# First attention of a Flamingo-like kernel: scores in two row halves, masks of four heads, maximum subtracted on VectorE

## The reference

```
def _feature_map(x, fm_w, fm_b):
    z = jnp.einsum('nshd,ed->nshe', x, fm_w) + fm_b
    return jnp.concatenate([jnp.exp(z), jnp.exp(-z)], axis=-1)   # 8 -> 16 per head
# query = layernorm(x): 128 rows; keys = values = context: 77 rows; 16 heads
v, k, q = (_feature_map(x, fm_w, fm_b) for x in (v, k, q))
scores = jnp.einsum('nqhd,nkhd->nhqk', q, k) / jnp.sqrt(jnp.float32(EMBED))
attn = jax.nn.softmax(scores, axis=-1)
out = jnp.einsum('nhql,nlhd->nqhd', attn, v)
return out.reshape(N, S, HEADS * EXP_DIM) @ fc_w.T + fc_b
# x = x + tanh(g_xattn[0]) * (the above)
```

## Time and profile before

| | |
|---|---|
| three runs | 2557.52, 2557.7, 2568.71 us; median 2557.7 |
| profiled execution | 2560.78 us, span 2559.0 us |
| busy over the span | TensorE 2374.1 us (93%), VectorE 1993.7 (78%), ScalarE 1637.5 (64%), GpSimd 1541.8 (60%) |
| mean granted clock of TensorE | 0.947 of full speed |

### The profile page before, as it was taken

The page is one execution under the profiler, slowest core; times in us unless marked ns, Lnnn a source line. Parts: engine busy times, 40 slices in busy tenths (PEclk is TensorE's granted clock), DMA queues, the critical chain, the costliest instruction groups (busy, mean ns, idle before and its releaser), DMA issues. The chain is left out here.

```text
span 2559.0 us, 87168 instructions
## 1 busy us (share of the span) xinstructions
PE 2374.1 (93%) x29830; PEld 1817.8 (71%) x29830; DVE 1993.7 (78%) x4882; ACT 1637.5 (64%) x3917; POOL 1541.8 (60%) x1166
## 2 busy tenths in 40 slices
PE   4999999969599999999985999999999996699999
PEld 3888888847366666666654888888888886466666
DVE  6999999969788888888885666656565666888888
ACT  4888888834356555555654666666666653488887
POOL 2333333325366666666655777777777762488888
PEclk9999999955799999999997999999999996799999
DMA  2000000020422222222214333333343431000000
GB/s 75 6 5 5 6 5 6 4 66 0 87 88 82 86 83 79 87 80 86 76 34 104 63 63 59 64 58 66 57 67 57 67 58 39 3 10 12 12 12 17
DMA packets 411273, 123.96 MB, mean 48 GB/s; under 512 B 366195, under 2 KB 381171, under 8 KB 410432
## 3 DMA queue, kind: packets, MB, share of 16 engines
q1 hardware_dynamic: 278816, 89.38, 15.2%
q10 hardware_dynamic: 132384, 33.63, 5.9%
HBM read 109.03 MB, written 13.89 MB: 48 GB/s over the span
## 5 line engine op out<-in xcount | busy, mean ns | idle before, releaser
L1086 POOL TENSOR_TENSOR f_low<-f_hidden,f_high 128x512 f16<-128x512 f32 x336 | 442.5, 1322 | 250.4 <-ACT f_high L1021 248.6
L1044 DVE TENSOR_TENSOR f_hidden<-f_hidden,f_share 128x512 f32<-128x512 f32 x336 | 374.5, 1115 | 0.0
L1638 POOL TENSOR_TENSOR a_q_head_high<-a_q_t_high,a_head_mask 128x2048 f16<-128x2048 f16 x64 | 232.7, 3635 | 200.4 <-PE a_score L1424 192.3
L1230 POOL TENSOR_TENSOR f_low<-f_hidden,f_high 128x512 f16<-128x512 f32 x256 | 296.6, 1159 | 71.2 <-ACT f_high L1173 71.0
L398 POOL TENSOR_TENSOR a_kfeat<-a_feat,a_head_mask 128x616 f32<-128x616 f32 x128 | 154.1, 1224 | 302.2 <-ACT a_feat L333 302.2
L1027 ACT ACTIVATE f_act_out<-f_gate 128x512 f32<-128x512 f32 x336 | 200.4, 596 | 194.7 <-PE f_gate L991 194.7
L1067 DVE SCALAR_TENSOR_TENSOR f_hidden<-f_up,f_act_out 128x512 f32<-128x512 f32 x336 | 229.9, 684 | 83.0 <-PE f_up L991 59.8
L1021 ACT ACTIVATE f_high<-f_hidden 128x512 f16<-128x512 f32 x336 | 210.5, 627 | 73.0 <-DVE f_hidden L1044 71.6
L1573 ACT ACTIVATE a_prob<-a_score 128x308 f32<-128x308 f32 x256 | 109.4, 427 | 224.0 <-PE a_score L1432 224.0
L1730 DVE TENSOR_REDUCE a_score<-a_score 128x4 f32<-128x308 f32 x256 | 123.8, 484 | 161.9 <-PE a_score L1424 161.9
L1001 PE MATMUL f_y<-w_down_high,f_high 128*128 128x128 f16 x1344 | 242.4, 219 | 2.2 <-POOL f_low L1086 2.2
(11 more groups left out here) (273 smaller groups left out, 9327.0 us busy)
## 6 DMA issues: line engine op xcount, KB each, us to landing
f_share<-expert_shares SPq DMA_DIRECT2D x128, 256.0 KB, 3.2
a_q_pos<-queries ACTq DMA_DIRECT2D x64, 512.0 KB, 4.1
f_share<-expert_shares SPq DMA_DIRECT2D x128, 128.0 KB, 3.0
relative_values<-a_rel_all SPq DMA_DIRECT2D x1024, 4.0 KB
x_all<-in_x SPq DMA_DIRECT2D x4, 1024.0 KB, 7.7
f_share<-expert_shares SPq DMA_DIRECT2D x128, 32.0 KB, 1.8
queries<-a_q_parts SPq DMA_DIRECT2D x64, 64.0 KB, 3.5
a_rel<-relative_values SPq DMA_DIRECT2D x64, 64.0 KB, 1.9
```

The lines of the kernel that those rows point to most:

```text
L1044: nc.vector.tensor_tensor(hidden[r][:, :], hidden[r][:, :], share[k][:, :, :].rearrange("p t q -> p (t q)"), ALU.mult).then_inc(scaled, 1)
L1086: nc.gpsimd.tensor_tensor(low[r][:, :], hidden[r][:, :], high[r][:, :], ALU.subtract).then_inc(low_ready, 1)
L1230: nc.gpsimd.tensor_tensor(low[k][:, :], hidden[k][:, :], high[k][:, :], ALU.subtract).then_inc(low_ready, 1)
L1638: nc.gpsimd.tensor_tensor(q_head[p][k][:, :, :], q_t[p][k][:, :].unsqueeze(2).broadcast_to([P, P, NH]), head_mask[:, :].unsqueeze(1).broad ...
```

## The change

Row halves: rows 0 to 63 of a chunk hold four heads, rows 64 to 127 the other four. `own_mask`, the sum of the two halves of `head_mask`, lets kfeat be four heads wide instead of eight: each row keeps its head's place within its own half. One `scores(n, p, c)` then issues two matmuls that contract 64 rows each, in the two row halves of the array, into the two score banks. All four quarters get their maximum subtracted by VectorE into `prob`, and one exp each. `normalize` moves from VectorE to ScalarE, as scale and shift, where `layernorm_constants` makes the shift with one more instruction. The orders of all engines but GpSimd are written anew. One small operation and one count of `weights_ready` come before the loops.

```
-        kfeat = [sb(f"kfeat{p}", [P, 2, 8, KC]) for p in range(2)]
+        kfeat = [sb(f"kfeat{p}", [P, 2, HQ, KC]) for p in range(2)]
...
-                def scores(n, p, u):
-                    if inside(n, 0, B):
-                        if u % 2 == 0:
-                            pe.wait_ge(kfeat_ready, 2 * n + u // 2 + 1)
-                        wait(pe, exped, 4 * n + u - 1)
-                        c = u // 2
-                        nc.tensor.matmul(score_ps[u % 2][:, 0:QW], feat[p][:, c, 0:P],
-                                         kfeat[p][:, c, 4 * (u % 2):4 * (u % 2) + 4, :],
-                                         start=True, stop=True).then_inc(score_ready, 1)
+                def scores(n, p, c):
+                    if inside(n, 0, B):
+                        pe.wait_ge(kfeat_ready, 2 * n + c + 1)
+                        wait(pe, shifted, 4 * n + 2 * c)
+                        for r in range(2):
+                            own = slice(HALF * r, HALF * (r + 1))
+                            nc.tensor.matmul(score_ps[r][:, 0:QW], feat[p][own, c, 0:P], kfeat[p][own, c, :, :],
+                                             start=True, stop=True).then_inc(score_ready, 1)
...
                 def slot(n, p):        # TensorE
                     o = 1 - p
                     scores(n, p, 0)
-                    turn(n - 1, 2)
+                    turn(n - 1, 3)
+                    mix(n - 1, o, 1)
                     prep_z(n + 1, o)
-                    mix(n - 1, o, 0)
                     fin_project(n - 3, o)
                     scores(n, p, 1)
-                    turn(n - 1, 3)
                     prep_value(n, p)
-                    mix(n - 1, o, 1)
-                    scores(n, p, 2)
+                    mix(n - 1, o, 2)
                     turn(n, 0)
-                    mix(n - 1, o, 2)
+                    mix(n - 1, o, 3)
+                    turn(n, 1)
                     fin_turn(n - 2, p)
+                    turn(n, 2)
+                    mix(n, p, 0)
                     prep_turn(n + 2, p)
-                    scores(n, p, 3)
-                    turn(n, 1)
-                    mix(n - 1, o, 3)
...
                 def exp(n, u):         # ScalarE
                     if inside(n, 0, B):
-                        act.wait_ge(shift_ready, 4 * n + u + 1)
-                        if u in ON_DVE:
-                            last = nc.scalar.activation(prob[u][:, :, :], prob[u][:, :, :], ACT.Exp, scale=SCALE)
-                        else:
-                            wait(act, prob_ready, 4 * n + u - 3)
-                            for h in range(HQ):
-                                last = nc.scalar.activation(prob[u][:, h, :], score_ps[u % 2][:, KC * h:KC * (h + 1)],
-                                                            ACT.Exp, bias=shift[u][:, h:h + 1], scale=SCALE)
-                        last.then_inc(exped, 1)
+                        act.wait_ge(shifted, 4 * n + u + 1)
+                        nc.scalar.activation(prob[u][:, :, :], prob[u][:, :, :], ACT.Exp, scale=SCALE).then_inc(exped, 1)
...
+                def normalize(n, p):
+                    if inside(n, 0, B):
+                        wait(act, xn_t, n - 1)
+                        nc.scalar.activation(xn[p][:, :], x_all[:, n, :], ACT.Identity, bias=xn_shift[:, n, :],
+                                             scale=rstd[:, n, :]).then_inc(xn_ready, 1)
...
                 def slot(n, p):        # ScalarE
                     o = 1 - p
                     high_prob(n - 1, 2)
+                    copy_xn(n + 1, o)
+                    high_prob(n - 1, 3)
+                    exp(n, 0)
+                    exp(n, 1)
                     features(n + 1, o)
-                    exp(n, 0)
-                    high_prob(n - 1, 3)
                     high_value(n, p)
-                    exp(n, 1)
                     high_prob(n, 0)
                     exp(n, 2)
-                    copy_xn(n + 2, p)
                     high_prob(n, 1)
+                    exp(n, 3)
                     copy_mixed(n - 2, p)
-                    exp(n, 3)
+                    normalize(n + 3, o)
...
+                def subtract_max(n, u):        # VectorE
+                    if inside(n, 0, B):
+                        s = score_ps[u % 2][:, 0:QW].rearrange("q (h k) -> q h k", h=HQ)
                         dve.wait_ge(top_ready, 4 * n + u + 1)
+                        wait(dve, prob_ready, 4 * n + u - 3)
+                        nc.vector.tensor_tensor(prob[u][:, :, :], s, top[u][:, :].unsqueeze(2).broadcast_to([P, HQ, KC]),
+                                                ALU.subtract).then_inc(shifted, 1)
...
                 def slot(n, p):        # VectorE, as it is after the change
+                    inverse_sum(n - 2, p)
+                    divide(n - 2, p)
                     row_max(n, 0)
+                    row_max(n, 1)
+                    subtract_max(n, 0)
+                    subtract_max(n, 1)
                     low_prob(n - 1, 2)
                     residual(n - 3)
                     low_prob(n - 1, 3)
+                    statistics(n - 3)
+                    row_max(n, 2)
+                    row_max(n, 3)
+                    subtract_max(n, 2)
+                    subtract_max(n, 3)
+                    low_value(n, p)
                     low_prob(n, 0)
                     low_prob(n, 1)
```

More of the change, by code:

```diff
@@ L142, in _, with feature_attention @@
                         nc.vector.bn_stats(stats[:, n, :], x_all[:, n, :])
-def feature_attention(nc, B, io, x_all, stats, mean, rstd, ident, gates):
+def feature_attention(nc, B, io, x_all, stats, mean, rstd, xn_shift, ident, gates):
     with ExitStack() as ctx:
+        own_semaphores = []
         def sb(n, s, d=F32):
@@ L176, in feature_attention @@
         mixed_t = [sb(f"mixed_t{p}", [P, 2, P]) for p in range(2)]
-        top, shift = ([sb(f"{n}{k}", [P, HQ]) for k in range(4)] for n in ("top", "shift"))
+        top = [sb(f"top{k}", [P, HQ]) for k in range(4)]
         prob = [sb(f"prob{k}", [P, HQ, KC]) for k in range(4)]
@@ L192, in feature_attention @@
         value_t, value_high, value_low = sem("value_t"), sem("value_high"), sem("value_low")
-        score_ready, top_ready, shift_ready, exped = sem("score_ready"), sem("top_ready"), sem("shift"), sem("exped")
+        score_ready, top_ready, shifted, exped = sem("score_ready"), sem("top_ready"), sem("shifted"), sem("exped")
         prob_ready, prob_high, prob_low = sem("prob_ready"), sem("prob_high"), sem("prob_low")
@@ L232, in prep_z @@
                         if isinstance(n, int) and n == 0:
-                            pe.wait_ge(weights_ready, 4)
+                            pe.wait_ge(weights_ready, 5)
                         for c in range(2):
@@ L371, in slot @@
                     high_prob(n - 1, 2)
+                    copy_xn(n + 1, o)
+                    high_prob(n - 1, 3)
+                    exp(n, 0)
+                    exp(n, 1)
                     features(n + 1, o)
-                    exp(n, 0)
-                    high_prob(n - 1, 3)
                     high_value(n, p)
-                    exp(n, 1)
                     high_prob(n, 0)
                     exp(n, 2)
-                    copy_xn(n + 2, p)
                     high_prob(n, 1)
+                    exp(n, 3)
                     copy_mixed(n - 2, p)
-                    exp(n, 3)
-                act.wait_ge(weights_ready, 4)
-                slots(act, -2, LO, HI, LAST, slot)
+                    normalize(n + 3, o)
+                act.wait_ge(weights_ready, 5)
+                slots(act, -3, LO, HI, LAST, slot)
             @block.gpsimd
@@ L398, in slot @@
                             nc.gpsimd.tensor_tensor(
-                                kfeat[p][:, c, :, :], feat[p][:, c, P:P + KC].unsqueeze(1).broadcast_to([P, 8, KC]),
-                                head_mask[:, :].unsqueeze(2).broadcast_to([P, 8, KC]), ALU.mult).then_inc(kfeat_ready, 1)
+                                kfeat[p][:, c, :, :], feat[p][:, c, P:P + KC].unsqueeze(1).broadcast_to([P, HQ, KC]),
+                                own_mask[:, :].unsqueeze(2).broadcast_to([P, HQ, KC]), ALU.mult).then_inc(kfeat_ready, 1)
                         nc.gpsimd.tensor_tensor(x_all[:, n, :], x_all[:, n, :], fc_b[:, :],
                                                 ALU.add).then_inc(x_biased, 1)
-                pool.wait_ge(weights_ready, 4)
+                pool.wait_ge(weights_ready, 5)
                 slots(pool, 0, LO, HI, B, slot)
@@ L413, in _ @@
                     w_sign[:, :].unsqueeze(2).broadcast_to([P, 2 * 8 * 2, HD]), ALU.mult).then_inc(weights_ready, 1)
+                nc.vector.tensor_tensor(own_mask[:, :], head_mask[:, 0:HQ], head_mask[:, HQ:2 * HQ],
+                                        ALU.add).then_inc(weights_ready, 1)
```

(30 more changed lines are left out.)

14 lines of the change are left out of this document (1 added, 13 removed).

## The result

The changed kernel took 2576.07 us (median of 4 runs, 2575.07 to 2578.87), the kernel before 2557.61: an estimated ratio of 1.0064, interval 1.0035 to 1.0092. It is slower, by 18.5 us or 0.7% in the medians. The mean granted clock is 0.947 in both, so the clock has no part in it. The forecast of 2569 was 7 us low, inside its range of 2540 to 2590, with the direction that it gave the most chance (slower, 0.42).

What follows compares the result with a forecast made beforehand. Nearly full engines tied by semaphores, then a VectorE-TensorE ring: slot 7.55 to 7.74, +11.8 us over about 62 slots, -0.5 at the start, from 2560.8 to 2572, less 3.1 for the median: 2569 us, range 2540 to 2590.

Steps and rivals of the forecast that it cites:

- What bounds it: First attention before: nearly full engines tied by semaphores; VectorE's shift stalls behind GpSimd's multiply, 0.68 us every second slot.
- The ring: VectorE and TensorE: next scores queue behind turn(n,2), which waits for low_prob(n,0); slot 7.55 to 7.74 us.
- two waits: VectorE idles each slot: row_max some 0.6 us for first scores, residual 0.17 us for fin_project's y.
- Pair 0.77, out 0.14: TensorE's two 64-row score matmuls take 0.77 us, leaving the divided array 0.14 us.
- B1 beside A2: TensorE keeps order A1, A2, B1, B2, so only one record of each half overlaps; pair 0.77 us.
- rival (b): Score matmuls all run side by side: pair 0.52, slot 7.57, +1 us, 2558 us; chance 0.20.
- the route by y: TensorE from first scores through turn, mix, prep_z and fin_project to y, which VectorE's residual needs, at 3.09 us.
- the residual's stall: VectorE's residual(n-3) waits 0.17 us for y, ready at 3.09 against VectorE's own 2.92.
- The rivals' y of 3.35 and 2.83: Time y reaches VectorE: 3.35 us if halves take turns (chance 0.25), 2.83 if all run side by side (0.20).
- The signs that I named: Even slots near 7.7, no 1.2 us VectorE instruction, row_max idle 0.6, residual 0.1 to 0.4, A's second record with B's first.
- Edits costed at nothing: ScalarE's fewer exps and added normalize, covered by VectorE's 6.98 us; GpSimd's halved kfeat, except some 0.5 us at first slot.
- rival c: The ring has slack and VectorE alone sets the slot: 6.98 us, -35 us, 2522 us; chance 0.20.

Runs made afterwards that it cites:

- experiment 8: Kernel before with each GpSimd mask multiply cut into two of 308 elements: 2537.54 us, ratio 0.994.
- experiment 4: Kernel before with the maximum subtracted on VectorE in all four quarters, one exp each, old orders and masks: 2530.56 us, ratio 0.9853.
- 6: Kernel before with all maxima subtracted on VectorE and normalize moved to ScalarE, old orders, whole rows: 2528.16 us, ratio 0.99.
- experiment 3: Changed kernel with scores as two matmuls over all 128 rows and eight-head masks: 2591.75 us, ratio 1.0092.
- 5: Changed kernel with the next slot's first scores issued ahead of turn(n,2), and whole-row scores with eight-head masks: 2531.8 us, ratio 0.9911.
- 1: Changed kernel with the next slot's first scores issued ahead of turn(n,2), row halves kept: 2526.5 us, ratio 0.9837.
- experiment 2: Changed kernel with exp(n,3) moved behind copy_mixed and normalize on ScalarE: 2576.14 us, ratio 1.0027.

## Why it came out so

The stage's length, from first to last statistics, in us:

| kernel | order | rows | stage |
|---|---|---|---|
| before | old | whole | 460.9 |
| 8: masks cut | old | whole | 440.9 |
| 4: all subtracted | old | whole | 430.2 |
| 6: and normalize on ScalarE | old | whole | 430.2 |
| 3: the change with whole rows | new | whole | 491.9 |
| the change | new | halves | 476.8 |
| 5: scores early | new, mended | whole | 430.9 |
| 1: scores early | new, mended | halves | 428.2 |

So the change is a sum of large parts: -30.7 for what its work does in the old orders (before to 6), +61.7 for the order (6 to 3), -15.1 for the halves with their shorter masks inside the ring (3 to the change). Together +15.9. The parts hold for this way through the table, since they depend on each other: out of the ring the halves are worth 2.7, not 15.1. The call's place is worth 61.0 of the order's 61.7 in whole rows (3 to 5) and 48.6 in halves.

**What bounds it: right.** The GpSimd stall behind the earlier trace rows was real and costs about what was read: 0.68 us every second slot is 21 us over 62 slots, and 20.0 went in experiment 8. The trace alone shows the two instructions ending together (248.82 + 1.24 = 250.06 and 248.81 + 1.21 = 250.02). The Trainium skill (SBUF — State Buffer, section "SBUF: two separate sides") says that GpSimd and certain VectorE instructions share a port pair under an exclusive lock, the loser waiting the whole instruction out. The end times and experiment 8, with its longest shift of 0.65 us, agree with that rule; no run separates it from another cause of the same timing.

**The ring: right, and it is the answer.** Its place, its members and its two waits were as predicted. From the rows above, each step from start to start, with the prediction's value behind it:
- first scores to row_max: 261.63 - 260.81 = 0.82 (0.73)
- two row_max and two subtractions: 263.18 - 261.63 = 1.55 (1.58)
- low_prob to residual: 263.87 - 263.18 = 0.69, a stall of 0.08 (0.61 and 0.17)
- residual to low_prob(n,0): 266.74 - 263.87 = 2.87 (2.94)
- low_prob(n,0) to turn(n,2): 267.56 - 266.74 = 0.82 (0.76)
- turn and mix: 268.34 - 267.56 = 0.78 (0.74)
- prep_turn and the entry: 268.60 - 268.34 = 0.26 (0.21)

The sum is 7.79, against 7.74.

**The size: the pair's price was off.** The term "Pair 0.77, out 0.14" was wrong. The next instruction starts 0.72 us after the start of the pair, not 0.91. The two fp32 matmuls of a pair run side by side from the start, and not only B1 beside A2. In the first 0.1 us of scores (268.60 to 268.70) two of the four records have begun in halves, in whole rows (268.11 to 268.20) one:

```profile
268.60 0.53 PE L253 MATMUL a_score<-a_kfeat,a_feat 64*128 64x308 f32 x2
```
```profile
268.11 0.42 PE L252 MATMUL a_score<-a_kfeat,a_feat 128*128 128x308 f32 x1
```

The other two start together as well, 0.36 us after the first two, so with 0.26 for a record I estimate 0.62 for the pair and 0.10 for leaving. That is rival (b)'s mechanism at a price above its 0.52, and its slot of 7.57 did not come. It counted only the route by y, and there other terms took the gain back: y was used at 263.87 - 260.81 = 3.06, not at 0.19 less than 3.09, because turn took 0.50 for 0.43, prep_z 0.78 for 0.70 (it stands behind mix now, in whole rows too) and fin_project 0.54 for 0.52. VectorE's own way there took 0.82 + 1.55 + 0.61 = 2.98 for 2.92. So the residual's stall only went from 0.17 to 0.08. The ring gave the rest back in small amounts: the first scores are seen 0.09 later, low_prob 0.06, turn with mix 0.04, prep_turn with the entry 0.05. Against that the pitches from row_max to low_prob(n,0) were 0.1 high in all. That 7.74 came within 0.05 of 7.79 is luck in part: errors of 0.24 one way met 0.19 the other. (The rivals' y of 3.35 and 2.83 add up to 3.36 and 2.84, which changes nothing.) The slot grew over 7.55 by 0.23 to 0.24, not 0.19: 14 to 15 us, not 11.8, and 15.9 in the stage. Of the 7.1 us missed, the profiled time holds 3.4 (2575.38 against 2572); the rest is that I took 3.1 off on the way to the median, where the changed kernel's median lies 0.7 above its profiled run.

The signs that I named came but for two: the residual's stall of 0.08 is under the 0.1 to 0.4, and the records start two by two.

The traces also price the divided array. In front of a pair fin_project takes 0.54 us with halves and 0.44 in whole rows (experiment 3), so entering costs 0.10, as put; prep_turn's 0.26 against 0.15 to 0.26 fits. Behind a pair the next instruction takes 0.06 more (turn 0.50 against 0.44, prep_value 0.28 against 0.22). A pair in halves thus costs 0.10 + 0.72 + 0.06 = 0.88 us of TensorE, against 1.03 to 1.04: half of the 0.31 that the pair alone shows is gone. The Trainium skill (TensorEngine Tiling (Array Packing), Key Properties) says that changing the tiling mode drains TensorE. On the way in the scores start 0.26 us after a prep_turn that lasts 0.31, so a full drain doesn't show (the profile models the ends of matmuls, so this is no proof), though the 0.10 may be part of one; on the way out at most 0.72 - 0.52 + 0.06 = 0.26 can be it. Its other rule (TensorE: Matmul & The Clock Gate, Part 3), that matmuls in distinct row groups are concurrent, agrees with the trace: four records in 0.79 us where whole rows need 1.20.

**Edits costed at nothing.** ScalarE's share stayed hidden: experiment 2 delays its last exp by 0.65 us and nothing moves. "VectorE alone sets the slot" (rival c, 6.98) was a real state, one call away: 6.95 in the mean came when the scores moved.

**What stays open.** Why the first scores are seen 0.82 us after their start in halves was not tried by itself. Two matmuls running side by side would both end late, which fits, but whole rows show 0.72 and 0.82 as well. Nor is it shown why experiment 4 is another 10.7 us shorter than experiment 8: it ends the GpSimd stall as 8 does, but also replaces the exps in four parts, and VectorE's waits for scores (22 us) and for high_prob (15 us) in 8 are gone in 4.

## What to carry to other kernels

Before believing an engine's busy sum, follow one item of work through the queues and ask what the next item's first instruction is queued behind. Here two engines with 11% of idle time each waited for one another, and moving a single call made +18 us into -41, each against the kernel before of its own series (2576.1 against 2557.6, 2526.5 against 2567.4). Test the order apart from the work in it: the same work took 430 or 492 us. And try the cheap part of a change alone: one constant gave -37 us, without any new order.

## What the runs showed of the hardware

Two fp32 matmuls of 64 rows and 308 columns in the two row halves take 0.72 us to the next instruction's start, against 1.03 for two of 128 rows; with entering (0.10) and what follows (0.06) the halves save about 0.15 us a pair. TensorE and VectorE can both show as busy 50.00 of 50 us while they pass every quarter's scores and probabilities between them (experiment 4). A four-element VectorE instruction took up to 1.24 us beside a GpSimd multiply of 616 elements, and 0.65 at most beside two of 308; cutting the multiply in two was worth 20 us. The releaser that a trace names for a wait on several semaphores can be a coincidence: exp(n,3) was named over 58 slots, and moving it behind the turn changed nothing.
